# Later load of the second layer's output weights, and next-head projections issued in pairs, in a two-layer recurrent kernel

## The reference

```python
# layer 0 mixer: linear attention, 16 query heads, 4 key/value heads, width 128
q, k = rope(x @ Wq.T), rope(x @ Wk.T); v = x @ Wv.T
qf, kf = elu(q) + 1, elu(k) + 1
state = state + k_s[..., :, None] * v_s[..., None, :]     # per token
num, den = q_s @ state, q_s . z + EPS;  out = num / den;  s = out @ Wo.T
# layer 0 feed-forward: 8 experts (top 2) and a shared one -> g
# layer 1 mixer: 32 heads of width 64 with a decaying state
states = states * dec + x_t outer b_t;  y = states @ c_t + x_t * D
y = y * silu(z); y = (y - mu) * rsqrt(var + EPS) * gamma + beta;  s = y @ W_out.T
# layer 1 feed-forward: quantized gate, up and down -> g
x = x + s * silu(g)
```

## Time and profile before

| | |
|---|---|
| three runs | 1802.15 us median (1801.72 to 1805.13) |
| profiled execution, its own time | 1803.97 us |
| its span in the profile | 1802.2 us |
| PE busy | 1652.1 us, 92% |
| DVE busy | 1153.2 us, 64% |
| ACT busy | 758.6 us, 42% |
| POOL busy | 664.2 us, 37% |
| mean granted TensorE clock | 0.969 of full speed |

### The profile page before, as it was taken

The page is one execution under the profiler, slowest core; times in us unless marked ns, Lnnn a source line. Parts: engine busy times, 40 slices in busy tenths (PEclk is TensorE's granted clock), DMA queues, the critical chain, the costliest instruction groups (busy, mean ns, idle before and its releaser), DMA issues.

```text
span 1802.2 us, 29615 instructions
## 1 busy us (share of the span) xinstructions
PE 1652.1 (92%) x11068; PEld 1370.2 (76%) x11068; DVE 1153.2 (64%) x2041; ACT 758.6 (42%) x1379; POOL 664.2 (37%) x500
## 2 busy tenths in 40 slices
PE   5997899898979999999969978998989899999988
PEld 3886677796868888887938866777968788888878
DVE  4334788653857777777753347886535677777767
ACT  3333455333434444444534334553334344444445
POOL 1454444101114555444514534441012155444535
PEclk9999999999989999999979989999999999999999
DMA  2333000001224443441023320000012343343410
GB/s 76 103 103 117 18 36 1 1 1 56 71 85 127 126 133 118 129 140 49 13 70 103 108 111 19 36 1 1 1 56 71 96 139 118 122 140 126 132 33 25
DMA packets 60061, 135.68 MB, mean 75 GB/s; under 512 B 8128, under 2 KB 12736, under 8 KB 59408
## 3 DMA queue, kind: packets, MB, share of 16 engines
q1 hardware_dynamic: 59920, 133.79, 23.6%
HBM read 130.81 MB, written 2.95 MB: 74 GB/s over the span
## 4 chain that ended last, share of the span: by engine, by line
PE 65%; DVE 11%; POOL 7%; issue 6%; ACT 6%; DMA 2%; SPq 1%; POOLq 0%; DVEq 0%; ACTq 0%
PE ps L550 29%; PE ps L607 6%; PE ps L869 4%; PE ps L893 4%; PE ps L646 4%; PE ps L831 3%; POOL silu_g L450 3%; PE ps L905 3%; PE ps L586 3%; POOL rb L468 2%; POOL fw_lo L435 2%; PE ps L880 2%; PE ps L748 2%; PE ps L599 2%; PE ps L749 2%
## 5 line engine op out<-in xcount | busy, mean ns | idle before, releaser
L550 PE MATMUL ps<-xnT_hi,w_in_hi 128*128 128x512 f32 x512 | 222.3, 434 | 0.0
L550 PE MATMUL ps<-xnT_lo,w_in_hi 128*128 128x512 f32 x512 | 203.0, 396 | 0.0
L550 PE MATMUL ps<-xnT_hi,w_in_lo 128*128 128x512 f32 x512 | 201.9, 394 | 0.0
L468 POOL TENSOR_TENSOR rb<-ra,rb 128x512 f32<-128x512 f32 x80 | 117.6, 1469 | 202.9 <-DVE rb L1532 202.9
L426 POOL TENSOR_TENSOR w_in_lo<-w_raw,w_in_hi 128x1024 fp32r<-128x1024 f32 x32 | 84.2, 2631 | 272.0 <-ACT w_in_hi L951 272.0
L1653 DVE TENSOR_TENSOR_SCAN lmat<-dec,ident 128x512 f32<-128x512 f32 x128 | 165.4, 1331 | 0.0
L1342 DVE TENSOR_TENSOR hid<-ps,silu_g 128x512 f32<-128x512 f32 (+1 forms) x80 | 55.1, 689 | 163.6 <-POOL silu_g L450 106.0
L513 POOL TENSOR_TENSOR yt<-yg,sz 128x512 f32<-128x512 f32 x64 | 82.1, 1283 | 172.9 <-ACT sz L1262 165.9
L550 PE MATMUL ps<-xnT_hi,fw_hi 128*128 128x512 f32 x312 | 127.9, 410 | 17.5 <-DVE fw_lo L1360 9.8
L435 POOL TENSOR_TENSOR fw_lo<-fw_raw,fw_hi 128x512 fp32r<-128x512 f32 (+1 forms) x56 | 62.6, 1119 | 185.3 <-ACT fw_hi L981 134.7
L550 PE MATMUL ps<-xnT_hi,fw_lo 128*128 128x512 f32 x312 | 125.6, 403 | 0.0
(11 more groups left out here) (194 smaller groups left out, 4392.8 us busy)
## 6 DMA issues: line engine op xcount, KB each, us to landing
dec<-dec_dram SPq DMA_DIRECT2D x64, 512.0 KB, 4.0
w_raw<-in_w_in SPq DMA_DIRECT2D x32, 512.0 KB, 4.8
wdec<-dec_dram SPq DMA_DIRECT2D x128, 128.0 KB, 3.9
pdec<-dec_dram SPq DMA_DIRECT2D x128, 128.0 KB, 3.7
fw_raw<-in_fw SPq DMA_DIRECT2D x40, 384.0 KB, 3.2
w_raw<-in_w_qkv SPq DMA_DIRECT2D x8, 768.0 KB, 4.2
comb<-comb_dram SPq DMA_DIRECT2D x8, 512.0 KB, 3.7
w_out<-in_w_o SPq DMA_DIRECT2D x2, 2048.0 KB, 10.7
```

The costliest lines, as they stand in the source:

```text
L468: nc.gpsimd.tensor_tensor(rb[:, k], ra[:, k], rb[:, k], ALU.add).then_inc(a_rot.sem, 1)
L550: mm = nc.tensor.matmul(out, left(l, k), right(r, k), start=(j == 0), stop=(j == len(steps) - 1))
```

## The change

The load of `w_out` moves from the end of phase 3 to the weights of pair h = 2, and SP no longer waits for the phase. `affine_sums` moves from feed-forward 1 to the end of DVE's state-space units 10 to 25, one t (two operations) in each. On ACT `ssm_prep(1, 1)` moves into the first unit, behind `xtok_copy`, and the Silu of `gate` is cut into eight of 256 columns, behind `z_silu` of units 0 to 7. In attention PE's projections are grouped 2 and 3, 4 and 5, 0 and 1, and DVE's list is changed to suit.

```diff
@@ sync
-                phase_over(b, 3)
-                sp.dma_start(w_out[:], a["w_out"]).then_inc(w_out_in, 16)
                 for k in range(2, NF1):
...
                     weights(split_ssm(b, h), a["w_in"][h], KT * XZBC)
+                    if h == 2:
+                        sp.wait_ge(o_mm.sem, o_mm.done(b * NC + NC - 1))
+                        sp.dma_start(w_out[:], a["w_out"]).then_inc(w_out_in, 16)
@@ tensor, att_head
                         att_score(n, c + 1)
                         if q_ahead:
                             att_project(*nxt, 2)
+                            att_project(*nxt, 3)
                         att_update(n, c)
                         att_numerator(n, c)
                         if q_ahead:
                             v_turn(*turn)
-                            att_project(*nxt, 3)
                         att_score(n, c + 2)
-                        if q_ahead:
-                            att_project(*nxt, 4)
                         att_update(n, c + 1)
                         att_numerator(n, c + 1)
                         if q_ahead:
                             k_turn(*turn)
+                            att_project(*nxt, 4)
                             att_project(*nxt, 5)
                         att_score(n, c + 3)
                         att_update(n, c + 2)
                         att_numerator(n, c + 2)
                         if kv_ahead:
                             att_project(n + 1, i + 1, hf, 0)
+                            att_project(n + 1, i + 1, hf, 1)
                         att_update(n, c + 3)
                         att_numerator(n, c + 3)
-                        if kv_ahead:
-                            att_project(n + 1, i + 1, hf, 1)
@@ scalar, ssm_unit
-                    if hf == 0 and 1 <= h and h + 1 < HP:
+                    if hf == 0 and h + 1 < HP:
                         ssm_prep(h + 1, (h + 1) % 2)
                     c_copy(u + 1)
                     btok_copy(u + 1)
                     z_silu(u)
+                    if u < 2 * b * HP + NC:
+                        c = u - 2 * b * HP
+                        if c == 0:
+                            act.wait_ge(f_sum.sem, f_sum.done(2 * b + 1))
+                        nc.scalar.activation(gate[:, c, :], gate[:, c, :], ACT.Silu)
...
-                ssm_prep(1, 1)
-                act.wait_ge(f_sum.sem, f_sum.done(2 * b + 1))
-                nc.scalar.activation(gate[:], gate[:], ACT.Silu)
@@ vector, att_head
                             rope_mul(*nxt, 2)
+                        mask(n, c + 2)
+                        if q_ahead:
                             feature(*nxt, 1)
-                        mask(n, c + 2)
+                        att_next_state(n, c + 1)
                         if q_ahead:
                             rope_mul(*nxt, 3)
                             feature(*nxt, 2)
-                        att_next_state(n, c + 1)
+                            rope_mul(*nxt, 4)
+                        mask(n, c + 3)
                         if q_ahead:
-                            rope_mul(*nxt, 4)
                             feature(*nxt, 3)
-                        mask(n, c + 3)
                         att_next_state(n, c + 2)
@@ vector, layer 1
                     decayed_scores(u + 1, 1)
+                    if b == 0 and 0 <= u - AFFINE_FROM < NT:
+                        affine_sums(u - AFFINE_FROM)
...
-                    if b == 0 and 3 <= u < 11:
-                        if u == 3:
-                            dve.wait_ge(w_out_in, 16 * 2)
-                        for t in range(2 * (u - 3), 2 * (u - 2)):
-                            affine_sums(t)
```

More of the change, by code:

```diff
@@ L54 @@
 SUFFIX = 8
+AFFINE_FROM = 10
 SH = 32
@@ L348, in ffn_weights @@
                 sp.dma_start(fw_raw[:, k % 2, :], src).then_inc(fw_in[k % 2], 16)
-            def phase_over(b, phase):
-                sp.wait_ge(phase_end, 4 * (b * PHASES + phase + 1))
             for j in range(NC // 2):
@@ L1712, in ssm_unit @@
                     decayed_scores(u + 1, 1)
+                    if b == 0 and 0 <= u - AFFINE_FROM < NT:
+                        affine_sums(u - AFFINE_FROM)
                 def affine_sums(t):
+                    if t == 0:
+                        dve.wait_ge(w_out_in, 16 * 2)
                     for x in range(2):
```

## The result

| | before | after |
|---|---|---|
| time, median | 1802.43 us (6 runs, 1796.65 to 1805.19) | 1814.09 us (6 runs, 1812.64 to 1817.1) |
| profiled execution, span | 1802.2 us | 1810.9 us |
| mean granted clock | 0.969 | 0.975 |

The ratio is 1.0068, 95% interval 1.005 to 1.0085: slower by some 12 us; the forecast was 1812 us. The first thing to take from the traces is a ledger: the same two instructions of PE's list are found in each trace, and their distances are compared (us). "Units" are the state-space units.

The account below looks back on a forecast made before the run. PE was taken as the bound in state-space units, with DVE's chain a near second in attention. 1803.97 + 29.4 - 12.7 - 6.9 = 1813.8, less 1.8 for the runs' median: 1812 us, range 1792 to 1828.

Parts of the forecast that it names:

- The loop in attention: Attention: moving projection 4 later closes a loop of waits through DVE, POOL, ACT and PE, 23.8 us per half-unit against 21.7.
- looser: Rival in attention: DRAM-free shadowing by masks lets DVE start rope 3 early, half-units stay 21.7 us, total 1782.6; chance 0.17.
- half closed: Rival in attention: only projection 4's direct delay counts, 14 x 1.3 = 18 us, total 1800.8; chance about 0.13.
- The stage's sum: Attention, both batches: seven half-units each lose 2.1 us, 14.7 per batch, 29.4 us in all; bounds 18 and 40.
- The clock's rival: Rival in attention: PE's clock falls behind the new waits in each of 14 half-units, 24 us more, 1836; chance 0.08.
- The weight parts on POOL: Attention, first half of a head: three weight parts between POOL's sums, guessed to lengthen the loop by 0.2 us on average.
- Start of the units: First state-space unit: PE's 4.58 us wait for ACT's copy of x goes, 6.3 us per batch, 12.7 in all.
- Feed-forward 1: Feed-forward 1 without affine sums: batch 0 comes down to batch 1's time, 6.9 us saved once; bounds 5 and 7.
- Alike in both batches: Sign to look for in the changed kernel's timeline: feed-forward 1 takes the same time in batch 0 and batch 1.
- Affine sums in units 10 to 25: State-space units 10 to 25: 15.3 us of added DVE work hides in DVE's 2.6 us pause per unit; cost 0.
- the rival of 1828 us: Rival in units 10 to 25: affine sums meet POOL and hold PE's chain 1 us per pair, 16 more; chance 0.10.
- the case as worked out: Whole kernel: the forecast with the closed attention loop and both gains, slower, between 1806 and 1822 us; chance 0.52.

Follow-up runs that it names:

- Number 5: Changed kernel with ACT's numerator copy ahead of `rope_act(1)`: 1795.8 us; with the value's copy also ahead of the key's two operations: 1788.72 us.
- number 4: Changed kernel with projection 4 alone put back behind the score of piece c+2: 1772.71 us, ratio 0.9843.

## Why the prediction was right, and where not

**The loop in attention: right in kind, and nearly in size.** The forecast of 23.8 us per half-unit measured 23.82 and 24.09 from rope to rope and 23.95 on average from score to score. That it is a loop and not a delay is shown by opening it at projection 4 (-41 us) and shortening it at the numerator's copy (-18). The rivals "looser" and "half closed" needed a half-unit under 23.1 and fall.

**The stage's sum: near the forecast partly by luck.** It came to +28.1 us for +29.4 (+30.7 where it was alone). From the first half-unit's score to the last one's, the seven half-units of a batch cost 16.4 and 16.2 us more than before, together 32.5. The rest of the stage gave back 4.4, which the prediction did not have: 1.5 and 1.1 us behind the last score, where the granted clock is 1.00 for 0.96 before, and 1.7 ahead of the first one in batch 1, which was not looked into.

**The clock's rival: not in the settled half-units, but once a batch.** Waits of 0.5 to 1.3 us, two or three a half-unit, left the granted clock at 1.00 in 211 to 320 us. In the seventh half-unit the longer wait of 2.94 us was followed by 0.50 for over 3 us, and this half-unit cost 4.6 us for the forecast 2.1.

**The weight parts on POOL: about right.** They were guessed at 0.2 us on average and cost 0.27 in every second round, 0.13 on average; the loop without them is 23.82 for 23.6. The bound for the case where all count does not follow as written: 24.8 us in each of 14 half-units would be 43 us, not 40. Number 5 missed by 5 us because its rounds at rope 3 are 22.54 and 22.83 us for the 22.3 expected; which link is the longer one was not traced.

**Start of the units: right**, 10.16 and 10.2 us for 10.15, -12.8 for -12.7, and -13.7 alone.

**Feed-forward 1: right in batch 0, with a miss in batch 1.** The sums' removal gave 7.67 for 6.9. Of this 4.5 is PE's waiting for hidT_lo (0.4 and 5.3 us before, 1.2 after); most of the rest is the low clock behind the long wait. "Alike in both batches" failed: batch 1 took 2.16 us more than before. PE comes to its last wait of the stage (the third row) 0.8 us sooner than before, and loses 1.2 us between there and the first x projection and 1.76 in the unit that follows:

```profile
1362.13 0.77 PE L549 MATMUL ps<-xnT_hi,fw_hi 128*128 128x512 f32 x1 [4.86 <-DVE fw_lo L1359]
...
1375.01 0.47 PE L549 MATMUL ps<-xnT_hi,fw_hi 128*128 128x512 f32 x1 [2.38 <-DVE fw_lo L1359]
...
1410.58 0.55 PE L585 MATMUL ps<-fw_hi,hidT_hi 64*128 64x256 f32 x1 [1.18 <-DVE hidT_lo L1350]
```

Its matmuls run at the lower level of the clock (1.2 GHz) from 1410.6 to 1417, which the window of that stretch shows (PEclk 0.50), where the kernel before has 1.00 (2.4 GHz) for the same work in 1397.8 to 1404.2. The wait of PE right ahead is the same in both, 1.18 and 1.16 us:

```profile
1410.60:1417.00 6.40, 6.40 (x21) 5.40 (x22) 3.55 (x5) 0.60 (x1) 0.00 (x0) 0.50 0.23 84
```

What differs is the stage ahead of it. In batch 1 of this kernel and of number 4, PE ends the wait of the second row 27.4 us into the stage, after 2.4 and 2.3 us for fw_lo. In every other feed-forward 1 of the 13 traces it gets past this place 1.4 to 2.5 us later, after 1.6 to 1.9 us for ACT's fw_hi. These two also have the slow unit (8.78 and 8.86 us; without affine sums the others take 7.0 to 7.1). Why the clock falls there was not tried and stays open.

**Affine sums in units 10 to 25: right at nothing, though they do meet POOL.** The rest of batch 0's units changed by 0.1 us in 315, and PE has no wait at all in 600 to 800 us; the rival of 1828 us falls. But DVE is busy with the sums for 24.3 us there, for the 15.3 forecast and 15.2 before. Their median is 0.482 us (0.479 before), but in seven of the units one operation takes 1.51 us, each time while POOL works. DVE's pause of 2.6 us a unit is wide enough for that.

**The load of w_out: right in the time, not in the size.** It now takes 10.4 us from issue to landing instead of 7.8, presumably because it meets the units' own loads, which was not tried; their dec loads stayed at 4.0 and no engine waits for either.

**The net** is near the forecast, 1810.9 us of span for 1812.0: -1.3 in attention (+3.1 in the half-units, -4.4 around them), -0.8 and +2.2 in feed-forward 1, and -1.2 in the units and the smaller stretches. The chance of 0.52 for the case as worked out was modest for a loop all of whose terms but one were read from rows.

## What to carry to other kernels

Before a producer is moved down an in-order list, follow its product through every engine's list: if the walk comes back to the new place, its length is the new period, and the distance that the producer moved says little about the price. Such a loop shows in a trace as two engines that each idle for the other once per round while neither is full, and one instruction put back ahead of the point where it closes gives all of it back (here 41 us, the pauses of the old order included, and the best version: 1772.71 us, 1.6% below the kernel before). Read the period at the instruction that closes the loop; between two other instructions the same period can look like a long and a short one, as the half-units here. Lists that are changed together are priced together: each alone gave nothing that the times show, and both, with projection 4 in its place, 7 us more.

## What the runs showed of the hardware

**In this kernel, operations of DVE and POOL that both read two tiles in SBUF hold each other.** DVE's feature takes 0.69 us alone. Where a POOL operation has started first, it takes 1.25 to 1.61 us (32 times in the changed kernel). Where the feature starts first (227.77 in the loop above), POOL's sum takes 1.77 to 1.80 us instead of 1.27 to 1.30 (18 times). Timeline of the changed kernel, one sum behind a feature and one ahead of it:

```profile
227.82 1.77 POOL L467 TENSOR_TENSOR rb<-ra,rb 128x512 f32<-128x512 f32 x1 [5.76 <-DVE rb L1531]
...
254.60 1.29 POOL L467 TENSOR_TENSOR rb<-ra,rb 128x512 f32<-128x512 f32 x1
...
255.12 1.32 DVE L1544 SCALAR_TENSOR_TENSOR qT<-rb,ra 128x512 f32<-128x512 f32 x1
```

The later feature begins at 255.12, the sum ends at 255.89, and the feature ends 0.55 after that, nearly its full length: the one waits for the other rather than sharing. DVE's products that read PSUM are not held: the one at 252.39 runs beside POOL's sum of 251.63 in 0.69 us, and all 36 first products of a rope that start during a POOL operation take 0.68 to 0.69. The Trainium skill ("GPSIMD Engine Reference", key points) has the contention with DVE instructions of two SBUF inputs; this trace agrees.
